# Standing VectorE's residuals, statistics and moments in pieces between the gelu blocks of a fused transformer's last stage

## The reference

```python
x = x + _layernorm(Y @ W_out.T)              # end of the state-space layer

def _L1_ffn_ref(x, W0, bias0, W1, bias1):    # 256 -> 1024 -> 256
    X = x.reshape(-1, H).astype(jnp.float16)
    D = jnp.dot(X.astype(jnp.float32), W0.T) + bias0
    D = jax.nn.gelu(D, approximate=False).astype(jnp.float16)
    E = jnp.dot(D.astype(jnp.float32), W1.T) + bias1
    return E.astype(jnp.float16).reshape(B, L, H)

x = x + _layernorm(_L1_ffn_ref(_layernorm(x), W0, bias0, W1, bias1))
```

## Time and profile before

| | |
|---|---|
| median of 3 timed runs | 1258.72 us (1257.88 to 1259.25) |
| the profiled execution's own time | 1264.43 us |
| its span, first to last instruction | 1262.4 us |
| mean granted TensorE clock | 0.932 |
| busy: PE, DVE, ACT, POOL | 1118.8 (89%), 871.2 (69%), 638.3 (51%), 382.5 us (30%) |
| loop over the four chunks | about 1182 to 1253 us of the span |

### The profile page before, as it was taken

The page is one execution under the profiler, slowest core; times in us unless marked ns, Lnnn a source line. Parts: engine busy times, 40 slices in busy tenths (PEclk is TensorE's granted clock), DMA queues, the critical chain, the costliest instruction groups (busy, mean ns, idle before and its releaser), DMA issues. The chain is left out here.

```text
span 1262.4 us, 31643 instructions
## 1 busy us (share of the span) xinstructions
PE 1118.8 (89%) x12161; PEld 918.2 (73%) x12161; DVE 871.2 (69%) x2188; ACT 638.3 (51%) x1449; POOL 382.5 (30%) x545
## 2 busy tenths in 40 slices
PE   5569998779979996677799999999999999999987
PEld 4546776657869895455558888888888888888776
DVE  6466997778846679785476677667766776664574
ACT  4434555331433585566544554555455545553654
POOL 3331123076710046681155026102610261000120
PEclk9779999687989998777899999999999999999998
DMA  7737885222279887453333333233342432232001
GB/s 176 188 116 209 222 227 193 100 76 89 79 257 416 305 304 266 132 180 112 109 98 93 93 116 114 88 90 118 111 157 89 118 111 92 87 104 79 1 18 51
DMA packets 77987, 176.17 MB, mean 140 GB/s; under 512 B 12615, under 2 KB 26183, under 8 KB 75271
## 3 DMA queue, kind: packets, MB, share of 16 engines
q1 hardware_dynamic: 71564, 157.09, 38.8%
q0 software_dynamic: 6272, 17.05, 4.5%
HBM read 112.82 MB, written 61.08 MB: 138 GB/s over the span
## 5 line engine op out<-in xcount | busy, mean ns | idle before, releaser
L2394 ACT ACTIVATE decay<-masked,negcum 128x128 f32<-128x128 f32 x512 | 163.0, 391 | 102.3 <-DVE mixT L2458 102.3
L2302 PE MATMUL joint<-xh,w_high 128*128 128x512 f32 x512 | 209.2, 409 | 2.0 <-POOL wl L2238 2.0
L2302 PE MATMUL joint<-xl,w_high 128*128 128x512 f32 x512 | 200.2, 391 | 0.0
L2302 PE MATMUL joint<-xh,wl 128*128 128x512 f32 x512 | 199.9, 390 | 0.0
L2506 DVE COPY cT<-joint 128x512 f32<-128x512 f32 x128 | 88.3, 690 | 86.0 <-PE joint L2302 85.7
L2412 ACT ACTIVATE bT<-joint 128x512 f32<-128x512 f32 x128 | 76.7, 599 | 130.0 <-PE joint L2302 130.0
L2458 DVE TENSOR_TENSOR mixT<-pcb,decay 128x512 f32<-128x512 f32 x128 | 82.3, 685 | 54.0 <-PE pcb L2318 53.9
L2235 POOL TENSOR_TENSOR w_high<-w_in,none 128x512 fp32r<-128x512 f32 x32 | 35.0, 1094 | 261.1 <-DMA w_in<-in_w_bc 250.5
L2302 PEld LDWEIGHTS joint<-xh,w_high 128*128 128x128 f32 x512 | 96.1, 188 | 23.7 <-POOL wl L2238 2.4
L2302 PEld LDWEIGHTS joint<-xh,wl 128*128 128x128 f32 x512 | 96.1, 188 | 20.7
L2302 PEld LDWEIGHTS joint<-xl,w_high 128*128 128x128 f32 x512 | 96.3, 188 | 17.0
(11 more groups left out here) (369 smaller groups left out, 2731.5 us busy)
## 6 DMA issues: line engine op xcount, KB each, us to landing
cumrow<-ssm_cum SPq DMA_DIRECT2D x128, 256.0 KB, 3.3
slots_in<-blank SPq DMA_DIRECT2D x16, 1024.0 KB, 5.4
rows<-slots_in SPq DMA_DIRECT2D x32, 512.0 KB, 5.7
slots_out<-spare SPq DMA_DIRECT2D x32, 512.0 KB, 4.2
weights<-in_expert_quads SPq DMA_DIRECT2D x16, 768.0 KB, 9.0
w_in<-in_w_bc SPq DMA_DIRECT2D x32, 256.0 KB, 3.6
qk_parts<-parts SPq DMA_DIRECT2D x32, 192.0 KB, 2.3
stack<-qk_parts SPq DMA_DIRECT2D x32, 192.0 KB, 5.2
```

The source lines that it names most:

```text
L2302: last = nc.tensor.matmul(bank[:], w[:, j, col:col + P], a[:, k, c * CHUNK:(c + 1) * CHUNK], start=(m == 0), stop=(m == len(parts) - 1))
L2394: last = nc.scalar.activation(decay[:, n % 2, o], masked[:, n % 2, o], ACT.Exp, bias=negcum[:, c * TPC + i, head:head + 1])
```

## The change

VectorE's long blocks are cut. `statistics` becomes `stats` and `moments`, called apart; `add` does half of the tiles at a time. In a chunk that has a next one, the two halves of `add` stand behind casts 0 and 1, the `LN_X` statistics behind 2, their moments behind 3; the previous chunk's output statistics behind 4, its moments behind 5 and `add_end` behind 7; y's statistics behind 5 and its moments behind 6. The last chunk has the output statistics behind 1, moments behind 2 and `add_end` behind 4. `leave` waits for `add_end` of the chunk before, which reads the `y16` that it overwrites. GpSimd's `order` takes the output's norm before y's.

ScalarE's `normal_rows` move from behind gelu 3 and 4 to behind 5 and 6. `finish` moves to behind gelu 1 and 2, a chunk later than before; in the last chunk the second-last chunk's `finish` stands behind gelu 5 and 6 as before. TensorE's and SyncE's queues are as before.

```diff
--- before.py
+++ after.py
@@ -2563,7 +2563,7 @@
 
         order = [(LN_Y, 0), (LN_X, 0), (LN_Y, 1)]
         for g in range(NCH):
-            order += [(LN_X, g + 1)] * (g + 1 < NCH) + [(LN_Y, g + 2)] * (g + 2 < NCH) + [(LN_END, g - 1)] * (g > 0)
+            order += [(LN_X, g + 1)] * (g + 1 < NCH) + [(LN_END, g - 1)] * (g > 0) + [(LN_Y, g + 2)] * (g + 2 < NCH)
         order.append((LN_END, NCH - 1))
 
         def until(kind, g):
@@ -2714,9 +2714,11 @@
                 for g in range(NCH):
                     for n in range(NFH):
                         gelu(g, n)
-                        if n in (3, 4) and g + 1 < NCH:
-                            normal_rows((g + 1) * PAIRS_C + n - 3)
-                        if n in (5, 6) and g:
+                        if n in (5, 6) and g + 1 < NCH:
+                            normal_rows((g + 1) * PAIRS_C + n - 5)
+                        if n in (1, 2) and g > 1:
+                            finish((g - 2) * PAIRS_C + n - 1)
+                        if n in (5, 6) and g == NCH - 1:
                             finish((g - 1) * PAIRS_C + n - 5)
                     if g + 1 < NCH:
                         for b in range((g + 1) * PAIRS_C, (g + 2) * PAIRS_C):
@@ -2728,29 +2730,33 @@
             def _(dve):
                 link = linker(dve, chain)
 
-                def statistics(rows, kind, g):
+                def stats(rows, kind, g):
                     for i, row in zip(range(g * TPC, (g + 1) * TPC), rows):
                         last = nc.vector.bn_stats(norms["stats"][:, kind, i, :], row)
                     link(last)
+
+                def moments(kind, g):
                     measure(nc, link, norms, kind, range(g * TPC, (g + 1) * TPC)).then_inc(var_ready, 1)
 
                 def rows_of(src, g):
                     return [src[:, i, :] for i in range(g * TPC, (g + 1) * TPC)]
 
-                def of_y(g):
+                def y_stats(g):
                     dve.wait_ge(y_in, (g + 1) * PAIRS_C)
-                    statistics(rows_of(y, g), LN_Y, g)
-
-                def add(g):
-                    dve.wait_ge(rstd_ready, until(LN_Y, g))
-                    for i in range(g * TPC, (g + 1) * TPC):
+                    stats(rows_of(y, g), LN_Y, g)
+
+                def add(g, half):
+                    if half == 0:
+                        dve.wait_ge(rstd_ready, until(LN_Y, g))
+                    first = g * TPC + half * PAIRS_C
+                    for i in range(first, first + PAIRS_C):
                         last = nc.vector.scalar_tensor_tensor(x[:, i, :], y[:, i, :], rstd[:, LN_Y, i:i + 1],
                                                               x[:, i, :], ALU.mult, ALU.add)
-                    link(last)
-                    statistics(rows_of(x, g), LN_X, g)
-
-                def end(g):
-                    statistics([y16[:, i, :] for i in range(TPC)], LN_END, g)
+                    if half:
+                        link(last)
+
+                def end_rows():
+                    return [y16[:, i, :] for i in range(TPC)]
 
                 def add_end(g):
                     dve.wait_ge(rstd_ready, until(LN_END, g))
@@ -2768,6 +2774,8 @@
 
                 def leave(g):
                     dve.wait_ge(down_done, (g + 1) * NFH)
+                    if g:
+                        dve.wait_ge(end_added, g * TPC)
                     for i in range(TPC // 2):
                         last = nc.vector.tensor_tensor(y16[:, 2 * i:2 * i + 2, :], acc[i][:],
                                                        bias1[:].unsqueeze(1).broadcast_to([P, 2, D]), ALU.add)
@@ -2779,27 +2787,51 @@
                     nc.vector.tensor_tensor(wl[:, n, :], wraw[:, n, :], wh[:, n, :].bitcast(F32), ALU.subtract
                                             ).then_inc(w_split, 1)
 
-                of_y(0)
+                y_stats(0)
+                moments(LN_Y, 0)
                 for n in range(2):
                     low(n)
-                add(0)
+                for half in range(2):
+                    add(0, half)
+                stats(rows_of(x, 0), LN_X, 0)
+                moments(LN_X, 0)
                 for n in range(2, NFH):
                     low(n)
-                of_y(1)
+                y_stats(1)
+                moments(LN_Y, 1)
                 dve.wait_ge(loaded, 32)
                 for g in range(NCH):
                     for n in range(NFH):
                         hidden(g, n)
-                        if n == 0 and g + 1 < NCH:
-                            add(g + 1)
-                        if n == 1 and g + 2 < NCH:
-                            of_y(g + 2)
-                        if n == 2 and g:
-                            end(g - 1)
-                        if n == 4 and g:
-                            add_end(g - 1)
+                        if g == NCH - 1:
+                            if n == 1:
+                                stats(end_rows(), LN_END, g - 1)
+                            if n == 2:
+                                moments(LN_END, g - 1)
+                            if n == 4:
+                                add_end(g - 1)
+                            continue
+                        if n < 2:
+                            add(g + 1, n)
+                        if n == 2:
+                            stats(rows_of(x, g + 1), LN_X, g + 1)
+                        if n == 3:
+                            moments(LN_X, g + 1)
+                        if g:
+                            if n == 4:
+                                stats(end_rows(), LN_END, g - 1)
+                            if n == 5:
+                                moments(LN_END, g - 1)
+                            if n == NFH - 1:
+                                add_end(g - 1)
+                        if g + 2 < NCH:
+                            if n == 5:
+                                y_stats(g + 2)
+                            if n == 6:
+                                moments(LN_Y, g + 2)
                     leave(g)
-                end(NCH - 1)
+                stats(end_rows(), LN_END, NCH - 1)
+                moments(LN_END, NCH - 1)
                 add_end(NCH - 1)
 
 
```

## The result

In runs of both kernels on the same chip the median went from 1259.35 us (9 runs, 1257.88 to 1263.46) to 1252.97 us (9 runs, 1249.48 to 1256.53); ratio 0.9943, 95% interval 0.9927 to 0.9959. By the medians that is 6.4 us less, by the interval 5.2 to 9.2; forecast were 1252.2 us and 6.5 less. So the times show a gain of some us, and that the first medians meet the forecast to 0.1 is partly luck; how large the gain is must be read from the traces.

The account below looks back on a forecast made before the run. TensorE's gaps in the last stage's loop, mostly down-blocks waiting for VectorE's casts, were taken as the bound. Removing six gains 6.5 us, everything added counts 0: 1258.72 to 1252.2 us, range 1250.8 to 1256.4.

Parts of the forecast that it names:

- The sum: Last stage's loop: TensorE's six waits for VectorE's cast cost 5.0 + 6 x 0.26 = 6.56 us, taken as 6.5.
- check by length: Excess of chunks 0 to 2 over a chunk without gaps, less the gelu table's load: together 6.4 us.
- the table's load: ScalarE's load of the gelu table ahead of the first gelu: a 1.3 us TensorE wait the change leaves alone.
- The walk: VectorE's queue through chunk 1, the fullest: no cast late, smallest margin 0.5 us; read-out behind `add_end` has margin 0.27.
- The turn: TensorE's transposes for the next chunk, due at 13.25 us; second normalised pair ready about 13.3, due 13.69, margin 0.4.
- Rival (a): Gaps move to the turn: three turns each 1.9 us late, 5.7 in all, 1257.9 us; chance 0.13.
- Rival (b): Each VectorE piece between two casts costs TensorE 0.45 us, 9.9 lost against 6.5 won: 1262.1 us; chance 0.04.
- Rival (c): Loop faster but end not earlier, or the same waits remain: 1258.7 us; chance 0.06.
- The price of the rows' move: ScalarE's normalised rows behind gelu 5 and 6: gelu 6 starts at 10.97 instead of 10.62 us, within margins, no cost.

Follow-up runs that it names:

- Blocks kept: Changed kernel with VectorE's undivided blocks and GpSimd's order as before; loop 71.44 us, median 1259.29 us, ratio to before 0.9990.
- the extra statistics: Changed kernel plus statistics of four x tiles into an unread tile behind cast 4 of chunks 0 to 2: loop 64.87 us; three such: 69.88 us.

## Why the prediction was right

- **The sum.** Six gaps at their shown idle time plus 0.26 each, 6.56, taken as 6.5; the loop lost 6.60. The shown idle time alone would have given 5.0. Read from start times, the six gaps of before cost 6.58: their first matmuls start 5.94 late in all, and the matmul behind each a further 0.10 or 0.11. The prediction's check by length came near, at 6.4, with two slips that nearly cancel: its chunk 0 begins 0.36 behind the chunk's first matmul (1181.95 for 1181.59), and it took the table's load at the shown 1.3 instead of 1.5. Blocks kept shows that these gaps are what VectorE's blocks cost, with all six in one kernel and none in the other.
- **The walk.** VectorE's timeline of the changed kernel in chunk 1, which starts at 1194.65:

```profile
1204.17 0.43 DVE L2773 CAST hid<-act 128x512 fp32r<-128x512 f16 x1 [0.19 <-DVE norm_stats L2735]
...
1205.06 1.40 DVE L2735 BATCH_NORM_STATS2 norm_stats<-y 128x6 f32<-128x256 f32 x4
1206.50 0.43 DVE L2773 CAST hid<-act 128x512 fp32r<-128x512 f16 x1
...
1208.55 0.43 DVE L2773 CAST hid<-act 128x512 fp32r<-128x512 f16 x1 [1.06 <-ACT act L2697]
1208.89 1.67 DVE L2765 SCALAR_TENSOR_TENSOR x<-y,norm_rstd,x 128x256 f32<-128x256 f16 x4
1210.86 0.69 DVE L2780 TENSOR_TENSOR y<-joint,bias 128x512 f16<-128x512 f32 x1 [0.30 <-PE acc L2648]
```

  Casts 5, 6 and 7 start at 9.52, 11.85 and 13.90 (9.51, 11.86, 13.93 foretold), `add_end` at 14.24 (14.27), and the read-out waits for TensorE, not for `add_end`: VectorE has 0.30 to spare there (0.27 foretold).
- **The turn.** ScalarE's timeline of the changed kernel, same chunk, and below it TensorE's:

```profile
1203.39 0.69 ACT L2697 ACTIVATE act<-ph,bias 128x512 f16<-128x512 f32 x1 [1.19 <-PE ph L2634]
1203.98 1.08 ACT L453 ACTIVATE xn<-x,norm_shift,norm_rstd 128x256 f16<-128x256 f32 x2
...
1205.63 0.67 ACT L2697 ACTIVATE act<-ph,bias 128x512 f16<-128x512 f32 x1
1206.20 1.08 ACT L453 ACTIVATE xn<-x,norm_shift,norm_rstd 128x256 f16<-128x256 f32 x2
1207.31 0.63 ACT L2686 ACTIVATE xn<-xn 128x512 f32<-128x512 f16 x1
```

```profile
1207.89 1.04 PE L2620 MATMUL turned<-ident,xn 128*128 128x128 f32 x8
```

  The second pair is ready at 1207.94, 0.05 after the turn begins; the turn's first half, on the first pair, covers it. Rival (a) did not come about in the changed kernel. The margin was 0.4, as put, and gelu 6 started 10.98 into the chunk (10.97 foretold).
- **Rival (b)**, 0.45 for each piece, falls with the changed kernel's list, which has no wait for a cast, and with the extra statistics: one more piece in each of three chunks costs 0.03 us in all.
- **Rival (c)**, a shorter loop with no earlier end, falls too: 9.3 us lie between the last down-block and the end of the span before and after, and both intervals of the ratio exclude 1.
- **The price of the rows' move.** The prediction put it at nothing, and no wait came of it. What it did not say is what the move saves: left out, 5.5 of the 6.6 us are lost. Most of the gain needs both edits.

## What to carry to other kernels

For work slipped between the steps of a pipeline, write when each step's output is due and when it will be done. In this loop such work was free until the first lateness and then cost all of it, so that the place where a block starts mattered and how finely it is cut did not. When a piece moves later, move every consumer that stands in an in-order queue ahead of other work. To price a gap on TensorE, take start times: here the six lost 0.26 us each beyond their shown idle time, and one of 0.23 was not shown at all.

## What the runs showed that I had not expected

Time ahead of the loop varied by 6.6 us between profiles with nearly the same queues there (1175.5 to 1182.1), as much as the whole gain. GpSimd's power for four tiles took 1.11 us at the median in the loop of before and 1.01 in all nine of the changed kernel. The nine traces part the two cleanly: the 32 powers of the loops and tails that began while VectorE was inside a cast took 1.11 to 1.37, the other 49 took 1.01, and 21 of those had a whole cast begin and end within them. So what goes with the longer time is a cast under way at the power's start, not one beside it; why was not tested.
